# An attention and feed-forward layer on one core: identity turned first, first tile ahead, feed-forward splits moved into the projection, last tile in halves

## The reference, cut to what matters

```python
x = x + layernorm(attention(layernorm(x)))          # latent attention, 32 heads, causal
x = x + layernorm(ffn(layernorm(x)))
# ffn:
def qlora_linear(x, wq, A, B):
    return x @ tile(wq, (1, 4)).T + (x @ A.T @ B.T) * 0.5
gate = silu(qlora_linear(x, w1q, a1, b1))           # hidden width 1376
up   = qlora_linear(x, w3q, a3, b3)
out  = qlora_linear(gate * up, w2q, a2, b2)         # rank 2 in A and B
```

## Time and profile before

| | |
|---|---|
| median of three runs | 589.05 us (586.78 to 589.89) |
| profiled execution | 590.17 us |
| its span, first to last instruction | 588.2 us |
| mean granted clock of TensorE | 0.992 |
| TensorE matmuls busy | 559.6 us (95% of the span) |
| VectorE busy | 448.8 us (76%) |
| ScalarE busy | 393.7 us (67%) |
| GpSimd busy | 196.2 us (33%) |

### The profile page before, as it was taken

One profiled execution on the slowest core, in us unless ns is written; L12 is line 12 of the kernel. 1 busy time (PEld: TensorE's weight loads), 2 busy tenths in 40 slices (PEclk: granted clock), 3 DMA queues, 4 the chain that ended last, 5 costly groups with the idle time before them and its releaser, 6 DMA issues. The chain is left out here.

```text
span 588.2 us, 10811 instructions
## 1 busy us (share of the span) xinstructions
PE 559.6 (95%) x3272; PEld 425.5 (72%) x3272; DVE 448.8 (76%) x1203; ACT 393.7 (67%) x1160; POOL 196.2 (33%) x204
## 2 busy tenths in 40 slices
PE   4998999999999999999999999999899999988995
PEld 4766778777787787787788788776588888644564
DVE  4878787787787777777877877879677889786466
ACT  4566778787787787787877877877543553534343
POOL 2225354344444543543453453440000000044520
PEclk9999999999999999999999999999899999998998
DMA  8711223212312322231111111024560000010003
GB/s 342 286 74 50 78 71 106 78 51 93 111 50 79 107 70 78 65 111 37 53 55 32 51 48 40 20 75 167 211 267 1 1 0 1 32 45 10 1 19 125
DMA packets 19560, 46.91 MB, mean 80 GB/s; under 512 B 2608, under 2 KB 3120, under 8 KB 19248
## 3 DMA queue, kind: packets, MB, share of 16 engines
q1 hardware_dynamic: 19504, 46.23, 22.8%
HBM read 39.80 MB, written 6.42 MB: 79 GB/s over the span
## 5 line engine op out<-in xcount | busy, mean ns | idle before, releaser
L721 DVE CUSTOM_DVE_ANT_0 ss<-bank,cst 128x128 f32<-128x128 f32 (+3 forms) x256 | 125.2, 490 | 73.1 <-PE bank L1065 40.9
L444 ACT ACTIVATE pt<-bank 128x128 f32<-128x128 f32 (+3 forms) x256 | 109.8, 429 | 61.5 <-PE bank L1115 61.3
L436 ACT ACTIVATE pr<-ss,small 128x128 f32<-128x128 f32 (+3 forms) x256 | 142.4, 556 | 4.7 <-DVE small L721 2.0
L338 POOL TENSOR_TENSOR qrot<-qrot,qswp 64x512 f32<-64x512 f32 x64 | 81.9, 1280 | 119.1 <-DVE qrot L713 116.7
L1115 PE MATMUL bank<-ident,pr 128*128 128x128 f32 x640 | 113.7, 276 | 1.6 <-ACT pr L436 1.5
L1115 PEld LDWEIGHTS bank<-ident,pr 128*128 128x128 f32 x640 | 78.4, 141 | 23.5 <-ACT pr L436 5.9
L345 POOL TENSOR_TENSOR qt_lo<-qrot,qt_hi 128x384 fp32r<-128x384 f32 x64 | 64.7, 1010 | 65.2 <-ACT qt_hi L426 64.0
L1063 PE MATMUL bank<-kt_hi,qt_hi 128*128 128x256 f32 (+2 forms) x192 | 80.8, 421 | 0.3 <-DVE small L721 0.3
L1127 PE MATMUL bank<-pt,kvn 128*64 128x256 f32 (+3 forms) x512 | 75.5, 437 | 0.7 <-ACT pt L444 0.7
L1127 PEld LDWEIGHTS bank<-pt,kvn 128*64 128x64 f32 x512 | 34.8, 137 | 43.5 <-issue 32.6
L1065 PE MATMUL bank<-kt_hi,qt_lo 128*128 128x256 f32 (+2 forms) x192 | 65.1, 339 | 0.0
(11 more groups left out here) (172 smaller groups left out, 1101.3 us busy)
## 6 DMA issues: line engine op xcount, KB each, us to landing
rsb<-rinv_scratch SPq DMA_DIRECT2D x64, 128.0 KB, 2.9
sq<-sq SPq DMA_DIRECT2D x16, 448.0 KB, 3.4
sv<-sv SPq DMA_DIRECT2D x10, 576.0 KB, 4.7
wv_raw<-wvo_scratch SPq DMA_DIRECT2D x8, 512.0 KB, 4.1
sve<-sv SPq DMA_DIRECT2D x6, 576.0 KB, 10.7
wvo_scratch<-vs SPq DMA_DIRECT2D x11, 256.0 KB, 2.4
xa<-x SPq DMA_DIRECT2D x8, 256.0 KB, 4.8
x<-x SPq DMA_DIRECT2D x1, 2048.0 KB, 9.4
```

The costliest lines, as they stand in the source:

```text
L338: nc.gpsimd.tensor_tensor(qrot[RKV:P, h, :], qrot[RKV:P, h, :], qswp[RKV:P, h, :], ALU.add)\
L436: nc.scalar.activation(pr[:, k % 4, 0:n], ss[:, RING[k], 0:n], ACT.Exp, bias=negmax[:, k % 8:k % 8 + 1], scale=-1.0, accum_out=rsum[:, k:k ...
L444: nc.scalar.activation(pt[:, b, h, 0:i + 1, i * P:(i + 1) * P], bank[2 + k % 2][:, 0:(i + 1) * P].rearrange("p (j q) -> p j q", q=P), ACT. ...
L721: nc.vector.tensor_tensor_reduce(out=ss[:, RING[k], 0:n], in0=bank[k % 2][:, 0:n], in1=mask[:, SEQ - n:SEQ], scale=-SCALE, scalar=3.4e38, ...
```

## The change

- TensorE turns the identity 18 times into an unused bank before the first tile.
- The first tile's high part is made between the second and third of the four high parts of `wa`; its low part in VectorE's iteration 0, behind the statistics of tile 1; its product with `wa` in TensorE's iteration 1, ahead of the turn of tile 1.
- In the projection `xf_lo` of the first batch moves from iteration 7 to 6, splits 3 to 6 into iteration 7, and splits 7 to 11 follow the `gu` of groups 0 to 4. The last tile's second square root and scale move from group 1 into the projection, ahead of the first Silu; of the dots of tile 6 the last one moves behind the statistics of tile 7.
- The turn of the last tile, its copies and the high part of the second batch's activations come one group earlier (8 to 7 on TensorE, 9 to 8 on ScalarE). The down weights' high part moves from group 8 to 12, their low part from 11 to 14, the two steps of `b2` from 7 and 8 to 16 and 18.
- The down part's last tile is computed in two halves of 256 columns (the second half in another bank), with statistics by halves, two halves of `z2`, of the sum and of the transfer. VectorE's sum of tile 6 moves ahead of the statistics of tile 7.

```diff
+WARM = 18
+HALVES = (slice(0, D // 2), slice(D // 2, D))
...
+    def y_bank(t, j=0):
+        return bank[UP[0] if j else YB[t % 3]]
...
             for t in range(TB):
-                sp.wait_ge(g.out_made, t + 1)
-                sp.dma_start(ob[t], yo[:, t % 2, :]).then_inc((g.out_sent0, g.out_sent1)[t % 2], 16)
+                for j, cols in enumerate(HALVES if t == TB - 1 else (slice(0, D),)):
+                    sp.wait_ge(g.out_made, t + 1 + j)
+                    sp.dma_start(ob[t][:, cols], yo[:, t % 2, cols]).then_inc(
+                        g.out_sent2 if j else (g.out_sent0, g.out_sent1)[t % 2], 16)
...
                 if t == 0:
                     act.wait_ge(f.wa_in, 16)
                     for k in range(DC):
+                        if k == 2:
+                            turned_hi(0)
                         nc.scalar.activation(wa_hi[:, k, :], wa[:, k, :], ACT.Copy).then_inc(f.wa_hi_made, 1)
...
-                if 0 <= t - 1 < TB - 1:
+                if 0 <= t - 1 < TB:
                     second_deviation(t - 1)
...
                     if G == 1:
-                        second_deviation(TB - 1)
                         normalise_sum(TB - 1)
...
-                    if G == 9:
+                    if G == 8:
                         move_turned(TB - 1)
                         lora_hi(TB - 1)
                         act.wait_ge(c.xt2_moved, TB)
                         nc.scalar.activation(xf_hi[:, SEQ:TOK], xft[:, SEQ:TOK], ACT.Copy).then_inc(g.xf_hi_made, 1)
-                    if G == 8:
+                    if G == 12:
                         act.wait_ge(g.wd_in, 16)
                         nc.scalar.activation(wd_hi[:, :, :], wd[:, :, :], ACT.Copy).then_inc(g.wd_hi_made, 1)
...
-                    if G == 7:
+                    if G == 16:
                         act.wait_ge(g.b2_in, 16)
                         nc.scalar.activation(b2_s[:, :], b2[:, :], ACT.Copy).then_inc(g.b2_hi_made, 1)
...
-                nc.scalar.activation(z2[:, t % 2, :], bank[YB[t % 3]][:, :], ACT.Identity, scale=st3[:, t % 2, 9:10],
-                                     bias=st3[:, t % 2, 10:11]).then_inc(g.z_made, 1)
+                for j, cols in enumerate(HALVES if t == TB - 1 else (slice(0, D),)):
+                    nc.scalar.activation(z2[:, t % 2, cols], y_bank(t, j)[:, cols], ACT.Identity,
+                                         scale=st3[:, t % 2, 9:10], bias=st3[:, t % 2, 10:11]).then_inc(g.z_made, 1)
...
                 if t + 1 < TB:
                     moments(t + 1)
+                if t == 0:
+                    turned_lo(0)
...
                     if u:
-                        lora_dots(u - 1, (2, 3))
+                        lora_dots(u - 1, (2, 3) if t < TB else (2,))
...
                     statistics(st2, x1[:, u, :], c.dve_step)
+                    if t == TB:
+                        lora_dots(u - 1, (3,))
+                    second_scale(u)
+                    if t + 1 < TB:
+                        split_output(t + 1, 0)
+                    if t == 7:
+                        for n in range(3, 7):
+                            split_gate(n)
                     if t < TB:
-                        second_scale(u)
-                        if t + 1 < TB:
-                            split_output(t + 1, 0)
                         fold_sum(u)
                         lora_dots(u, (0, 1))
...
-                if t == 7:
                     dve.wait_ge(g.xf_hi_made, 1)
                     nc.vector.tensor_tensor(xf_lo[:, 0:SEQ], xft[:, 0:SEQ], xf_hi[:, 0:SEQ].bitcast(F32), ALU.subtract)\
                       .then_inc(g.xf_split, 1)
...
-                    if G + 3 < 12:
-                        split_gate(G + 3)
-                    if G == 1:
-                        second_scale(TB - 1)
+                    if G + 7 < 12:
+                        split_gate(G + 7)
...
-                    if G == 11:
+                    if G == 14:
                         dve.wait_ge(g.wd_hi_made, 1)
                         nc.vector.tensor_tensor(wd_lo[:, :, :], wd[:, :, :], wd_hi[:, :, :].bitcast(F32), ALU.subtract)\
                           .then_inc(g.wd_split, 1)
-                    if G == 8:
+                    if G == 18:
 
                         dve.wait_ge(g.b2_hi_made, 1)
...
+            for t in range(TB):
+                st = st3[:, t % 2, :]
+                if t < TB - 1:
                     dve.wait_ge(g.y_made, t + 1)
                     nc.vector.bn_stats(st[:, 0:6], bank[YB[t % 3]][:, :]).then_inc(g.moments_raw, 1)
                     dve.wait_ge(g.moments_raw, t + 1)
                     nc.vector.bn_aggr(st[:, 6:8], st[:, 0:6]).then_inc(g.moments_made, 1)
...
+                else:
+                    add_sum(t - 1)
+                    for j in range(2):
+                        dve.wait_ge(g.y_made, t + 1 + j)
+                        nc.vector.bn_stats(st4[:, j, :], y_bank(t, j)[:, HALVES[j]]).then_inc(g.moments_raw, 1)
+                    dve.wait_ge(g.moments_raw, t + 2)
+                    nc.vector.bn_aggr(st[:, 6:8], st4[:, :, :]).then_inc(g.moments_made, 1)
+                if 0 < t < TB - 1:
+                    add_sum(t - 1)
...
+            for j in range(2):
+                add_sum(TB - 1, j)
...
             pe.wait_ge(f.ident_made, 1)
+            for _ in range(WARM):
+                nc.tensor.transpose(bank[7][:, 0:P], ident[:, :], ident[:, :])
...
+                if t == 1 or 1 <= t - 2 < TB:
+                    latents(max(t - 2, 0))
...
-                    if G == 8:
+                    if G == 7:
                         turn_y(TB - 1)
```

More of the change, by code:

```diff
@@ L191, in build @@
     st3 = ff3.take("st3", [P, 2, 16])
+    st4 = ff3.take("st4", [P, 2, 6])
     bank = [nc.alloc_psum_tensor(f"bank{i}", [P, 512], F32) for i in range(8)]
@@ L552, in _ @@
                     move_early(t - 1)
[L553 to L559 removed]
+                if 1 <= t - 1 < TB:
+                    turned_hi(t - 1)
                 if 0 <= t - 4 < TB:
@@ L1037, in _, with add_sum @@
             lora_down_lo(1)
-            for t in range(TB + 1):
-                if t < TB:
-                    st = st3[:, t % 2, :]
+            def add_sum(u, j=0):
+                cols = HALVES[j] if u == TB - 1 else slice(0, D)
+                dve.wait_ge(g.z_made, u + 1 + j)
+                if u >= 2 and j == 0:
+                    dve.wait_ge((g.out_sent0, g.out_sent1)[u % 2], 16 * (u // 2))
+                nc.vector.tensor_tensor(yo[:, u % 2, cols], x1[:, u, cols], z2[:, u % 2, cols], ALU.add)\
+                  .then_inc(g.out_made, 1)
+            for t in range(TB):
+                st = st3[:, t % 2, :]
+                if t < TB - 1:
                     dve.wait_ge(g.y_made, t + 1)
@@ L1204, in body, with latents @@
                         query(2 + k, 1, k)
+            def latents(u):
+                pe.wait_ge(f.xt_split, u + 1)
+                if u >= 2:
+                    pe.wait_ge(f.qn_made, u - 1)
+                for k in range(DC):
+                    if u == 0:
+                        pe.wait_ge(f.wa_split, k + 1)
+                    last = three(bank[2 + u % 2][:, 0:LAT], xt_hi[:, u % 4, k, :], xt_lo[:, u % 4, k, :],
+                                 wa_hi[:, k, :], wa_lo[:, k, :], k == 0, k == DC - 1)
+                last.then_inc(f.lat_made, 1)
             pe.wait_ge(f.ident_made, 1)
+            for _ in range(WARM):
+                nc.tensor.transpose(bank[7][:, 0:P], ident[:, :], ident[:, :])
             for t in range(TB + 4):
@@ L1352, in _ @@
                     pe.wait_ge(g.z_made, t - 2)
-                for r in range(RT):
-                    n = RROWS[r]
-                    three(bank[YB[t % 3]][:, :], fs_hi[0:n, hf, r, q:q + P], fs_lo[0:n, hf, r, q:q + P], wd_hi[0:n, r, :],
-                          wd_lo[0:n, r, :], r == 0, False)
-                nc.tensor.matmul(bank[YB[t % 3]][:, :], l2[:, hf, q:q + P], b2_s[:, :], start=False, stop=True)\
-                  .then_inc(g.y_made, 1)
+                for j, cols in enumerate(HALVES if t == TB - 1 else (slice(0, D),)):
+                    for r in range(RT):
+                        n = RROWS[r]
+                        three(y_bank(t, j)[:, cols], fs_hi[0:n, hf, r, q:q + P], fs_lo[0:n, hf, r, q:q + P],
+                              wd_hi[0:n, r, cols], wd_lo[0:n, r, cols], r == 0, False)
+                    nc.tensor.matmul(y_bank(t, j)[:, cols], l2[:, hf, q:q + P], b2_s[:, cols], start=False, stop=True)\
+                      .then_inc(g.y_made, 1)
 def kernel(**inputs):
```

55 lines of the change are left out of this document (19 added, 36 removed).

## The result

The changed kernel takes 594.46 us (median of 5 runs, 591.76 to 595.27) beside 589.5 for the kernel before in the same session: ratio 1.0079, 95% interval 1.0052 to 1.0105. It is slower by 0.8%; I had forecast 590.3 and a range up to 593.0.

The account below looks back on a forecast made before the run. TensorE was taken as busy nearly everywhere, so its waits and the halved clock behind long gaps counted. Terms -0.6 -2.2 -1.7 +0.6 +2.8 +1.2 +0.5 +0.7 = +1.3 on the median 589.05 gave 590.3, range 585.4 to 593.0.

Parts of the forecast that it names:

- The clock in the new gaps: Feed-forward: half-speed TensorE behind new gaps ahead of group 3 (+0.6) and at group 17 (+1.2).
- the walk through the first half: Feed-forward's first half: following VectorE's list, the second batch starts at 534.3 instead of 536.45, -2.2 (-1.2 to -3.5).
- Start: Kernel start: identity turns and first tile's product ahead bring the square root forward, -0.6 (0 to -1.5).
- identity of no use: Rival at the start: identity turns don't raise the clock, first term only -0.1, 590.8 in all; chance 0.18.
- Clock in the first half: Ahead of group 3: a gap of 2.2 may drop the clock, costing 1.2, taken at half, +0.6 (0 to 1.7).
- clock falls in both new gaps: Rival: the clock falls at group 3 and group 17, staying low 3.4 us each, 592.5 in all; chance 0.25.
- Clock ahead of the second batch: Before the second batch: gap 0.4 instead of 2.87, so the clock holds, -1.7 (0 to -1.8).
- Group 17: Second half: early down-weight split stalls the first a2 product, +2.8 (0 to 2.8), plus clock fall +1.2 (0 to 1.7).
- no stall: Rival at group 17: the stall doesn't come, as the addition doesn't interfere and VectorE has caught up, 585.9; chance 0.26.
- b2 and tail: b2 steps at group 18 make TensorE wait, +0.5 (0 to 1.0); last tile's later statistics, +0.7 (+0.2 to +1.1).

Follow-up runs that it names:

- e4: Changed kernel with identity turns filling three TensorE gaps (ahead of group 3, the last turn and group 17's a2 product): 589.98 us, ratio 1.0019.
- e13: Changed kernel with identity turns in five gaps (start, wv, group 3, last turn, group 17), so the clock is held: 589.84 us.
- e9: e8 with identity turns in three gaps (8 ahead of the first product, 20 ahead of wv's, 18 ahead of group 3): 583.54 us, ratio 0.9909.
- after: The changed kernel itself, as in the diff, without further edits: 594.46 us, ratio 1.0079 against the kernel before.
- e11: Changed kernel with only b2's low part back from group 18 to 17: 592.36 us, ratio 1.0057.
- e10: Changed kernel, last tile still in halves, but their statistics ahead of the sum of tile 6: 592.5 us, ratio 1.0062.
- e8: Changed kernel with the down weights' and b2's low parts at group 17, last turn behind group 8 and the old tail: 585.11 us, ratio 0.9922.
- e2: Changed kernel without the identity turns at the start (WARM = 0): 594.92 us, ratio 1.0097.
- e14: e13 with the last turn behind group 8 and that gap's filler dropped: 587.36 us.
- e12: Kernel before with only identity turns added, 14 ahead of wv's product and 9 ahead of the second batch: 588.31 us, ratio 0.9989.
- e3: Changed kernel with the down weights' low part at group 17 instead of 14: 589.8 us, ratio 1.0009.
- e1: Kernel before with only the change's start (identity turns, first tile's parts and product ahead): 586.51 us, ratio 0.9963.
- e15: e13 with the down weights' low part at group 17 and that gap's filler dropped: 586.86 us.
- e17: e13 with b2's low part at group 17: 588.75 us, ratio 0.9991.
- e16: e13 with the last tile's square root back behind the first Silus and group 3's filler dropped: 590.80 us.
- e18: e9 with the last tile in halves and their statistics ahead of tile 6's sum: 583.08 us, ratio 0.9888.

## Why the prediction was wrong, step by step

**In short.** The forecast was 590.3 and the median 594.5. Two steps failed. The clock in the new gaps stood in the sum with 0.6 and 1.2, 1.8 in all; holding it gives 4.5 (e4). And the walk through the first half (-2.2) came out 1.4 short with the clock held, of which the hold-up of two small copies by GpSimd's addition is 0.94 by the trace.

**The account.** From e13 to e9 four edits are undone: 2.5 + 3.0 + 1.1 + 0.9 (the last from the profiles) = 7.5, measured together 6.3. So the medians leave 1.2 over. The profiles close most of it: the turn takes 2.4 from its stage, the two splits share room on VectorE and take 2.75 and 0.89 singly but 3.16 together, and the tail takes 0.85, in all 6.4. Above e13, after has 4.6 of clock (less by up to 1, if its median is high as said at e11). Against the 589.2 of before (29 runs) stand these 4.6 and the 6.3 on the one side, and on the other what e9 is faster by, 5.7: the start, the square root, the splits put earlier and the clock.

**Start: direction right, size wrong.** I took 0.6 (0 to 1.5). The RMS step came 2.1 earlier, and the attention ended at 412.73 in this profile (414.86 before). The step that failed is "I take 0.6, between the two": I had left open whether the turns bring the higher clock, and let the product begin at about 8.2 at either. The turns did bring it and the product began at 7.51. By the end of the attention 0.5 to 2.2 are left in the profiles: 2.0 to 2.2 where the clock held (e10, e4), 0.5 to 1.3 where it fell again between 8 and 15 (e11, e8). The Trainium skill (TensorE: Matmul & The Clock Gate, Part 4, PE-mode transpose) says transposes don't bring the full clock; here 1.09 against 0.66 for the same four turns, and the filled gaps of e4, speak against it. My rival "identity of no use" is thereby refuted as a mechanism; what the turns are worth in the kernel's time is not shown (e2: 0.5, within the noise).

**First half: the term -2.2 failed.** The wait ahead of the second batch went, as forecast (2.87 to 0.42). But "dot 3 ... is there before the addition: 524.5, and its copies 524.8" took the copies for free of GpSimd. The dot did come before the addition, but the copies took 1.19, as the addition of 522.59 went ahead of them. I had applied the addition's hold-up to large operations and not to two copies of 12 columns. TensorE waited 2.19 ahead of group 8, and e14 shows the early turn gave nothing for it. With the clock held the stage is 0.8 shorter than before (29.40), where the term said 2.2, and 3.2 shorter with the turn behind group 8 (27.01).

**Clock in the first half: failed in number.** I priced one fall at half a chance of 1.2 (+0.6) and had none behind the last turn, for which I saw no long gap. Both came in the profile, and the stage is 2.8 longer than held (32.23 against 29.40): 0.8 to 1.2 for group 3, as priced, and 1.6 for the last turn. The rival "clock falls in both new gaps" had the mechanism, but for group 3 and group 17 only, at 592.5. The point I set for it (between 1.3 and 2.1 of idle) doesn't hold: falls followed gaps down to 1.41 (e12), and the clock held behind gaps of 2.25 and 2.40 for `wv` (after, e4), of 2.28 at group 3 (e3) and of 2.69 at group 17 (after).

**Clock ahead of the second batch: right.** -1.7 forecast, 1.57 in e1.

**Group 17: right.** +2.8 of stall against 2.69 in the trace and 3.0 in e15. I gave the fall 1.2 in the mean; e3 against e15 has 1.7 and the profiles 1.5, where it comes. The rival "no stall" is refuted.

**b2 and tail: right, low.** For b2 0.5 forecast, 0.85 in the trace, 1.1 in e17, just over the bound of 1.0. For the tail 0.7 forecast, 0.87 in the trace; its cause, the sum of tile 6 ahead of the statistics, is shown by e10.

**Square root ahead of Silu: not priced by itself.** I saw the gap ahead of group 3 (2.2 forecast, 2.27 in the trace) and the two table loads saved, and had no term for the edit alone. Once the clock is held it is worth 1.0 (e16). That this comes from the two loads is argued, not shown by a run of its own.

**Range and chances.** With "so falls seem not to come every time" I took one fall at half its price and the other at three quarters. For a median the likelier case counts in full: the four other runs of after have a lower clock than the profiled one and lie 2 to 3.5 above it. The upper end of 593.0 left no room for three gaps with a likely fall in each.

Open: which executions have which falls, and why; and what the turns at the start are worth in the kernel's time.

## What to carry to other kernels

A new wait of some 2 us ahead of TensorE is to be priced twice, as the wait and as half speed behind it (2.5 and about 1.6 to 2.0, 3.0 and about 1.5 to 1.7 here), unless something fills it. Turns of an identity into an idle bank cost nothing in the gap at group 17 (26.99 with and without them) and also make runs agree well enough to price single edits. At the start eight of them may cost some 0.5: the attention ends at 412.89 to 413.80 with them and at 412.68 to 412.82 in the profiles where the clock held without. A step is moved to where its engine waits anyway: the early split cost 3.0 at group 14; with it and b2's at 17 the stretch takes 23.82 (e9), 0.5 more than with both at their old places (23.33 in e1). Before a step that TensorE needs, follow what stands beside it on GpSimd, however small the step is, and give the turn of a tile the place where it is needed, not the earliest.

## What the runs showed of the hardware

- Turns of a 128x128 fp32 identity raised TensorE's clock and held it: 18 of them ahead of the first tile (e2 against after: 1.09 to 0.66 for four turns), and fillings in the gaps (granted clock 1.00 from 503 to 530 in e4; mean clock 0.996 to 0.999 in all 67 runs of e9 and e13 to e18, and 0.982 to 0.991 in those of after).
- The length of a gap alone does not decide: the clock fell behind 1.41 (e12) and held behind 1.56 (e1), 2.40 (e4) and 2.69 (after).
- After the early rise a gap of 1.41 ahead of the first product was followed by a second fall in some profiles and not in others; in e3 the window shows it:

```profile
9.00:15.00 6.00, 5.34 (x23) 0.57 1.04 413
```

- A stretch of products at half speed behind a gap costs less where another engine paces it: at most 1.0 behind `wv` (e9 against e8), and nothing in e12, since the wait comes back; 1.57 behind the gap ahead of the second batch (e1).
- Two copies of 128x12 took 1.19 instead of 0.25 beside a GpSimd addition, and the scaling of b2 1.40 instead of 0.49 (in the kernel before): operations that read one tensor in SBUF are held up too.
